# A graph layer's gathers in 342 slots and 61 rounds, a reordered first stage, and residual sums moved to DMAs

## What is computed

```python
# graph attention (GATv2), 4 heads of 64
h = rms_norm(xn) * rms_w @ W_down                   # 1250 x 256
src = concat(edge_src, arange(1250)); dst = concat(edge_dst, arange(1250))   # one edge to itself each
xl, xr = h @ Wl, h @ Wr
e = sum_d(att * leaky_relu(xl[src] + xr[dst]))      # per edge and head
alpha = softmax of e over the edges of one dst
gnn = segment_sum(alpha * xl[src], dst) @ W_up
# mixing without softmax
q, k, v = xn @ Wq.T + bq, xn @ Wk.T + bk, xn @ Wv.T + bv
mix = (q @ k.T * SCALE) @ v @ Wo.T + bo
x = x + gnn + mix
# feed-forward, weights and activations rounded to FP4 in blocks of 16
x = x + down(silu(gate(ln(x))) * up(ln(x)))
```

## Time and profile before

| | us |
|---|---|
| median of 3 runs | 925.71 (924.13 to 926.04) |
| profiled execution, its own time | 926.28 |
| its span, first to last instruction | 923.4 |
| TensorE busy | 854.8 (93%) |
| VectorE busy | 835.1 (90%) |
| ScalarE busy | 550.7 (60%) |
| GpSimd busy | 487.1 (53%) |

### The profile page before, as it was taken

How to read it: one execution, slowest core, us unless ns; L and a number is a source line. 1 busy time by engine, 2 the same in 40 slices (tenths; PEclk the granted TensorE clock), 3 DMA queues, 4 the chain that set the end, 5 groups by cost and what they waited for, 6 DMA issues and landing times.

```text
span 923.4 us, 9515 instructions
## 1 busy us (share of the span) xinstructions
PE 854.8 (93%) x2724; PEld 417.4 (45%) x2734; DVE 835.1 (90%) x1004; ACT 550.7 (60%) x1949; POOL 487.1 (53%) x512
## 2 busy tenths in 40 slices
PE   4999999999987999999999999999979988989664
PEld 3895455644433444444444444444434443444231
DVE  6989998779999999999999999999399689999994
ACT  3313123257767877879999978897388452343422
POOL 5200748577767767777777777877273100010101
PEclk8999999999997999999999999999999999999977
DMA  9322525553653533654335633339921210213124
GB/s 302 100 93 53 187 77 176 156 186 99 84 167 97 187 85 96 193 156 148 99 102 192 190 97 100 95 100 174 346 80 35 80 69 23 92 23 69 26 43 86
DMA packets 64850, 109.97 MB, mean 119 GB/s; under 512 B 29127, under 2 KB 35940, under 8 KB 64778
## 3 DMA queue, kind: packets, MB, share of 16 engines
q0 software_dynamic: 19856, 55.42, 24.3%
q1 hardware_dynamic: 44938, 53.92, 18.0%
HBM read 89.15 MB, written 17.17 MB: 115 GB/s over the span
## 4 chain that ended last, share of the span: by engine, by line
PE 72%; DVE 20%; SPq 2%; issue 2%; DMA 1%; ACT 1%; ACTq 0%; POOL 0%; DVEq 0%
PE acc L724 67%; DVE round_mem L1214 2%; DVE round_mem L1203 2%; SPq L515 2%; DVE round_mem L1204 2%; DMA big_b<-in_x 1%; PE turned L934 1%; DVE big_b L1556 1%; DVE round_mem L1207 1%; DVE round_mem L1208 1%; DVE z L1616 1%; PE turned L732 1%; DVE turned L1446 1%; PE turned L747 1%; DVE acc_sb L1454 1%
## 5 line engine op out<-in xcount | busy, mean ns | idle before, releaser
L552 POOL DMA_INDIRECT round_mem<-msg_table,idx x352 | 345.2, 981 | 102.1 <-issue 78.8
L1089 ACT ACTIVATE round_mem<-round_mem,pz 128x65 f32<-128x65 f32 x1408 | 353.9, 398 | 6.5 <-DVE acc_sb L1454 2.5
L724 PE MATMUL acc<-wslot,big_a 128*128 128x512 f32 x512 | 222.8, 597 | 7.9 <-DVE big_b L1411 7.9
L724 PEld LDWEIGHTS acc<-wslot,big_a 128*128 128x128 f32 x512 | 97.9, 192 | 131.2 <-issue 121.7
L1454 DVE TENSOR_REDUCE acc_sb<-round_mem 128x260 f32<-128x1820 f32 (+1 forms) x62 | 121.6, 1961 | 6.1 <-ACT round_mem L1089 4.0
L1079 ACT ACTIVATE pz<-z 128x7 f32<-128x7 f32 (+1 forms) x248 | 55.4, 296 | 107.9 <-DVE z L1621 107.7
L1446 DVE TENSOR_TENSOR turned<-round_mem,turned 128x1560 f32<-128x1560 f32 (+1 forms) x62 | 105.4, 1700 | 6.9 <-DMA round_mem<-msg_table,idx 4.6
L724 PE MATMUL acc<-wslot,big_b 128*128 128x512 f32 x256 | 110.0, 592 | 0.0
L724 PE MATMUL acc<-big_b,wslot 128*128 128x512 f32 x256 | 110.0, 592 | 0.0
L1616 DVE TENSOR_REDUCE z<-turned 128x24 f32<-128x1560 f32 (+1 forms) x62 | 105.1, 1695 | 2.1
L1614 DVE SCALAR_TENSOR_TENSOR turned<-turned,att_sb 128x1536 f32<-128x1536 f32 (+1 forms) x62 | 103.5, 1670 | 0.0
(11 more groups left out here) (232 smaller groups left out, 1022.9 us busy)
## 6 DMA issues: line engine op xcount, KB each, us to landing
big_b<-in_x SPq DMA_DIRECT2D x18, 512.0 KB, 9.9
round_mem<-msg_table,idx POOLq DMA_INDIRECT x352, 2.8
out_x<-big_b SPq DMA_DIRECT2D x9, 512.0 KB, 2.6
out_x<-acc_sb POOLq DMA_DIRECT2D x9, 512.0 KB, 5.4
wslot<-in_wv_t SPq DMA_DIRECT2D x2, 2048.0 KB, 9.2
wslot<-in_wk_t SPq DMA_DIRECT2D x2, 2048.0 KB, 9.4
wslot<-in_wo_t SPq DMA_DIRECT2D x2, 2048.0 KB, 9.4
wslot<-in_wq SPq DMA_DIRECT2D x2, 2048.0 KB, 9.9
```

The source lines that it names most:

```text
L552: pool.indirect_dma_start(xg[g % 4][:, j, :], None, msg_table, bass.IndirectOffsetOnAxis(idx[:, c, j0 + j:j0 + j + 1], 0)).then_inc(xg_in[ ...
L724: mm = nc.tensor.matmul(o(acc[:, n % 4, :]), a, b, start=first, stop=last)
L1089: ins = nc.scalar.activation(to[:, :, j], xg[g % 4][:, j, h * HR + 1:(h + 1) * HR], ACT.Copy, scale=pz[:, g % 2, j, h:h + 1])
```

## The change

Ten things change. (1) Slots: `CAPS`, so 342 slots in 61 rounds. (2) EARLY is 6 and not 7: two base groups move from before the tail into it. (3) The order of nodes is found by ScalarE (Sign with a sum, one instruction and a small one per block) between its takes of "lr"; each block's scatter starts when its rank is there. (4) VectorE and TensorE count the receivers earlier, and VectorE's order of weight pieces around that chain changes. (5) The small products "lin" go to a part of PSUM of their own and are no group. (6) GpSimd gathers the first block's receivers, then round 0's rows, then the other receivers. (7) The number of extra turns is worked out later in VectorE's order, by the same formula. (8) SP puts the bias row, and not x, into `base`; GpSimd adds x by accumulating DMAs (`add_x`) after its last gather. (9) GpSimd adds the mixing branch by accumulating DMAs (`lay_base`). (10) The plan of takes uses the round's size.

```diff
-EARLY = 7
+EARLY = 6
-CAPS = (54, 41, 38, 36, 34, 33, 32, 30, 28, 26)
+CAPS = (54, 40, 37, 35, 33, 32, 30, 29, 27, 25)
-PRODUCTS_AT, GROUP_STEP = 173.0, {"p0c": 2.0, "bias": 1.0}
-ROUND_0_AT, ROUND_STEP = 180.0, 8.5
+PRODUCTS_AT, GROUP_STEP = 172, {"p0c": 2.0, "bias": 1.0}
+ROUND_0_AT, SLOT_STEP, ROUND_OVER, TAKE_STEP = 160, 0.95, 2.2, 0.7
-BIAS_SUMS_AT, X_AT = 40, 54
+BIAS_SUMS_AT, X_AT = 43, 61
...
# SP
-            sp.wait_ge(acc_full, index_of["bias", 1] + 1)
+            sp.wait_ge(acc_taken["dve"], taken[index_of["bias", 1]])
             for c in range(C - 1):
-                sp.dma_start(base[:, c, :], x[c * NC:(c + 1) * NC, :]).then_inc(x_in[c], 16)
-            sp.wait_ge(mul_done, LAST + 1)
-            sp.dma_start(x_last, x[(C - 1) * NC:N, :]).then_inc(x_in[C - 1], 16)
+                sp.dma_start(base[:, c, :], bias_bc).then_inc(x_in[c], 16)
...
# GpSimd
-            pool.wait_ge(xr_out, 16)
+            pool.wait_ge(start_done, 1)
             for c in range(C):
                 pool.indirect_dma_start(neigh[:, c, :], None, src_table, ...)
             largest_weight(2)
+            pool.wait_ge(xr_out, 16)
+            receivers(0)
             pool.wait_ge(idx_done, 1)
             pool.wait_ge(table_out, 16)
             gather(0)
+            for c in range(1, C):
+                receivers(c)
+            pool.wait_ge(order_done, 2)
             rounds_over = pool.value_load(flags_i[0:1, 1:2], min_val=0, max_val=E)
             with pool.If(rounds_over > 0):
...
+                pool.dma_start(base[0:n, c, :], x[c * NC:c * NC + n, :], accum_op=ALU.add).then_inc(x_added[c], 16)
...
+                pool.dma_start(base[:, c, :].rearrange("p (k n) -> p k n", k=KB), base_at[c], accum_op=ALU.add).then_inc(base_added[c], 16)
...
# ScalarE
+            def rank(c):
+                nc.scalar.activation(is_above, key_row, ACT.Sign, scale=-1.0, bias=key_col[:, c:c + 1],
+                                     accum_out=rank_f[:, c:c + 1]).then_inc(ranked, 1)
+                act.wait_ge(ranked, c + 1)
+                nc.scalar.activation(rank_i[:, c:c + 1], rank_f[:, c:c + 1], ACT.Copy, scale=-0.5,
+                                     bias=0.5 * (NP - 1)).then_inc(rank_done, 1)
+            act.wait_ge(key_in, 32)
+            for c in range(3):
+                rank(c)
             for c in range(C):
                 take(index_of["lr", c])
+                if c + 3 < C:
+                    rank(c + 3)
...
# VectorE
-            for c in range(C):
-                step(nc.vector.tensor_scalar(is_above, key_row, key_col[:, c:c + 1], None, ALU.is_gt, ALU.add,
-                                             accum_out=rank_f[:, c:c + 1]))
-            nc.vector.tensor_copy(rank_i, rank_f).then_inc(rank_done, 1)
...
-            for c in range(min(LAST + 1 - X_AT, C - 2), C - 1):
-                add_bias(c)
-            dve.wait_ge(bias_added, C - 1)
-            for c in range(EARLY - 3):
-                add_base(c)
-            add_bias(C - 1)
```

More of the change, by code:

```diff
@@ L672, in rescale, with add_x, lay_base @@
                                         ALU.mult).then_inc(rescaled, 1)
+            def add_x(c):
+                n = rows(c)
+                if c < C - 1:
+                    pool.wait_ge(x_in[c], 32)
+                else:
+                    for i in range(C - 1):
+                        pool.wait_ge(x_in[i], 32)
+                pool.dma_start(base[0:n, c, :], x[c * NC:c * NC + n, :], accum_op=ALU.add).then_inc(x_added[c], 16)
+            def lay_base(c):
+                pool.wait_ge(acc_taken["act"], taken[index_of["base", ORDER["base"].index((c, 1))]])
+                pool.wait_ge(x_added[c], 16)
+                pool.dma_start(base[:, c, :].rearrange("p (k n) -> p k n", k=KB), base_at[c], accum_op=ALU.add).then_inc(base_added[c], 16)
             for g in range(1, LAST + 1):
@@ L686, in _ @@
                     send_attention(c)
+            for c in range(EARLY):
+                lay_base(c)
             def deviation_root(c):
@@ L956, in gps_layer @@
         round_of, freed, at = {}, {}, PRODUCTS_AT
-        for n in range(index_of["p", 0], len(groups)):
+        begun, n = ROUND_0_AT, index_of["p", 0]
+        for g, (_, _, slots, _, _) in enumerate(ROUNDS):
+            while n < len(groups):
+                kind, i, engine = groups[n]
+                full = max(at, freed.get(n - 4, 0)) + GROUP_STEP.get(kind, 7.0)
+                if full > begun:
+                    break
+                round_of[n], at = g, full
+                if kind == "base" and ORDER["base"][i][1] == 1:
+                    round_of[index_of["base", ORDER["base"].index((ORDER["base"][i][0], 0))]] = g
+                begun += TAKE_STEP if engine == "dve" else 0.0
+                freed[n] = begun + 0.8
+                n += 1
+            begun += ROUND_OVER + SLOT_STEP * slots
+            begun += 1.45 if g < KB or BIAS_SUMS_AT <= g < BIAS_SUMS_AT + KB else 0.0
+        for n in range(n, len(groups)):
             kind, i, _ = groups[n]
-            at = max(at, freed.get(n - 4, 0))
-            at += GROUP_STEP.get(kind, 7.0)
-            round_of[n] = max(0, math.ceil((at - ROUND_0_AT) / ROUND_STEP))
+            round_of[n] = LAST + 1
             if kind == "base" and ORDER["base"][i][1] == 1:
-                round_of[index_of["base", ORDER["base"].index((ORDER["base"][i][0], 0))]] = round_of[n]
-            freed[n] = max(at, ROUND_0_AT + round_of[n] * ROUND_STEP) + 1.5
+                round_of[index_of["base", ORDER["base"].index((ORDER["base"][i][0], 0))]] = LAST + 1
         def due(engine, g):
@@ L1550, in residual @@
             def residual(c, h):
-                if EARLY - 3 <= c < EARLY and (c, h) == min((i for i in x2_added if i[0] == c), key=x2_added.index):
-                    add_base(c)
+                if (c, h) == min((i for i in x2_added if i[0] == c), key=x2_added.index):
+                    if c < EARLY:
+                        dve.wait_ge(base_added[c], 16)
+                    else:
+                        dve.wait_ge(x_added[c], 16)
                 dve.wait_ge(x2_full, x2_made.index((c, h)) + 1)
@@ L1578, in sum_p0 @@
                 ins.then_inc(p0_summed, 1)
-            def add_bias(c):
-                n = rows(c)
-                dve.wait_ge(x_in[c], 32)
-                ins = nc.vector.tensor_tensor(base[0:n, c, :], x_last if c == C - 1 else base[:, c, :], bias_bc[0:n, :], ALU.add)
-                ins.then_inc(bias_added, 1)
-            def add_base(c):
-                dve.wait_ge(acc_taken["act"], taken[index_of["base", ORDER["base"].index((c, 1))]])
-                b = base[:, c, :].rearrange("p (k n) -> p k n", k=KB)
-                step(nc.vector.tensor_tensor(b, base_at[c], b, ALU.add))
-            assert round_of[index_of["bias", 1]] < X_AT
+            assert round_of[index_of["bias", 1]] + 3 < X_AT
             def sum_bias(k):
```

124 lines of the change are left out of this document (64 added, 60 removed).

## The result

The changed kernel takes **1182.17 us** (median of 4 runs, 1178.40 to 1183.14); the kernel before took 925.69 beside it. The ratio is 1.2801 (95% interval 1.2763 to 1.2840).

A forecast was written before the change was run, and what follows sets the result against it. TensorE and VectorE were taken as nearly full during the rounds. Round 0 at 432 after a 266 us turn, restart 465, last base group 967, first residual 971, tail 187: span 1158, forecast 1160 us, range 1125 to 1220.

The forecast's parts named there:

- The edges don't fit: Slots against caps: blocks 2 to 6, 8 and 9 each one short, so one extra turn runs through all ten blocks.
- no extra turn: Rival at the loop before round 0: slots miscounted, no turn runs, TensorE is the bound; 900 us, chance 0.08.
- The price of a block: One block's serial pass in the extra turn: 25.0 us of operations plus 1.5 for register waits, 26.5; 24 to 33.
- a block 38: Rival in the extra turn: register waits and fetches make each block 38 us; 1275 us, chance 0.07.
- Entering and leaving: Going into and out of the extra turn's loop: twice 5 us, between 0 and 15.
- VectorE reaches the loop: End of VectorE's first stage: at about 156 us instead of 174.3, since the ranks' 16 us leave VectorE.
- TensorE's restart: After the turn: TensorE goes on at 465 us, from round 0 at 432 plus 29 for three rounds plus 4.
- The products after it: TensorE from restart to last base group: 495 us for 72 groups, 4 for bias and small group, 3 for low clock.
- VectorE's rounds: VectorE from round 0 on: about 502 us, done at 938, beside TensorE, which ends later.
- "p" at 176: Start of TensorE's products: Gram begins some 2 us later because of ScalarE's ranks, so "p" begins at 176 us.
- The tail: From first residual to end of span: stays 187 us, with three add_base fewer and 4 us for two base groups.
- the DMA sums become the last wait: Rival at the first residual: it waits for bias, x and base sums on GpSimd's queue; +20, 1180 us, chance 0.05.

The follow-up runs named there:

- e1: Changed kernel with the number of extra turns forced to 0, so edges above the caps are left out of the result: 911.68 us, ratio 0.9866.
- e2: Changed kernel with the least caps that hold every edge (349 slots in 62 rounds): 910.54 us, ratio 0.9847.
- e3: Kernel before with only the new CAPS line of the change: 1185.63 us, ratio 1.2836.
- e6: e2 with one constant more, ROUND_0_AT = 172 for 160 in the plan of takes: 901.61 us, ratio 0.9762.
- e4: Changed kernel with the extra turn going only through the seven blocks short of a slot, every edge kept: 1102.08 us, ratio 1.1923.
- e8: Changed kernel with its turn and PRODUCTS_AT = 144 for 172, so p0 and p1 are taken in round 0, not round 3: 1169.00 us, ratio 1.2662.
- e9: e6 with EARLY 7, as before the change, in place of 6: 902.42 us, ratio 0.9787.
- e7: e6 with x, bias and mixing branch added by VectorE again as in the kernel before: 906.48 us, ratio 0.9811.

## Why the prediction was right

The direction, the mechanism and the size held: 1160 forecast, 1182 measured, inside 1125 to 1220. Point by point:

- **The edges don't fit: right.** e1, e2 and e3 show it from three sides. The rival "no extra turn" gave 900; e1, which is that rival, took 911.7. The rival took the plan to be on time, which e6 shows to be worth 8 us, and the tail to stay 187, where e1 has 190.9.
- **The price of a block: 26.5, measured 26.3** (27.15 for the first, 26.2 for each of the nine others), and 26.7 by e4. Two errors cancel by luck. The waits on register values, for which I added 1.5, cost nothing: gaps of a few hundredths of a us between VectorE's steps. The last reduction takes 3.4, where I took 2.05 from the rounds. The rival "a block 38" falls.
- **Entering and leaving: 10, measured next to nothing.** There are 0.21 us before the first instruction and 0.31 after the last. The 5.29 of the kernel before, where the loop is jumped over, are gone when it is run through, and are back as 6.46 in e2. The Trainium skill's rule (Runtime: NRT & Kernel Launch, Instruction fetch mechanics) is that a jump out of the fetched window waits for a fetch while straight code doesn't. The traces agree with it; they show where the gap stands, not the fetch itself. I had taken the sum to be 5 us lower by this rule; it was 10.
- **VectorE reaches the loop: 156, measured 171.** This step failed. I took the ranks' 16 us out and let the rest close up. But VectorE then waited: 5.1 for the places (at 108.7, forecast 106), 2.2 for GpSimd's maximum over the partitions, 7.2 for ScalarE's column sums (behind TensorE's Gram), and 4.2 for the receivers' rows, whose last gather GpSimd issued at 165.17, since they moved behind `gather(0)`; I had put their end near 150. So of 18 us only 3 came. The free entry (10) and the loop, 3 shorter than forecast, hide most of this: round 0 is at 434.9, against 432. That this is only 3 us off is luck.
- **TensorE's restart: 465, measured 469.7**, from p0 in round 3 as forecast. e8 shows why it is that late: the plan of takes, and not VectorE's time, held TensorE from 437 to 470.
- **The products after it: 502, measured 513.4.** This is the largest error that reaches the sum. I charged 3 us of low clock and nothing for late takes. The clock cost 2.5 (160 matmuls in 71.23 where 0.43 each would be 68.8), but TensorE waited 9.8 for ScalarE's takes of t1 and t2 on top, 6.1 of it ahead of the base groups. It waits so also without the turn (6.51 there in e2). The plan is part of the cause: with its constant moved, e6 waits 4.4 around the first base groups and nothing before them from 172 us on.
- **VectorE's rounds: about 502, measured 514.5** (434.9 to 949.4). The prediction's own terms make 510, not 502: the rounds before last 546 us (179.6 to 725.6), less 10, 2, 8.5 and 15.3. The gap from there to the end of the last base group is 33.7 us and not 29. Nothing of this reaches the sum, since TensorE came last.
- **"p" at 176, measured 172.7.** The 2 us later that I expected did not come; the products begin 1.7 sooner than before. TensorE then stands longer for it, and the sum doesn't change.
- **The tail: 187, measured 189.8.** The two base groups cost all of their 12.6 (e9), not 4, and the sums give back 4 to 5 (e7), about what I had for them. In steps: the other edits make the tail 6.2 shorter (e9), the two groups 12.6 longer (e6), and in the changed kernel it is 3.6 shorter than that, for a reason that is in part open. So the small error of 2.8 is luck.
- **The rival "the DMA sums become the last wait"** did not come. GpSimd issued the last `add_x` at 936.72 and the sum for block 3 at 957.07, each later one as soon as ScalarE had taken its groups. GpSimd of the changed kernel, in order of time, waits 12.20 and 12.38 for those takes, and its queue is otherwise free:

```profile
950.93 4.79 POOL L697 DMA_DIRECT2D big_b<-xhat_t  x3 [0.19 <-issue]
957.07 1.54 POOL L697 DMA_DIRECT2D big_b<-xhat_t  x1 [1.35 <-ACT xhat_t L1066]
970.80 1.54 POOL L697 DMA_DIRECT2D big_b<-xhat_t  x1 [12.20 <-ACT xhat_t L1066]
984.72 1.54 POOL L697 DMA_DIRECT2D big_b<-xhat_t  x1 [12.38 <-ACT xhat_t L1066]
```

The three sums of the first row, block 0's with them, were issued 31 us ahead of the first residual.

The measured 22 over the forecast are, in terms of the sum: round 0 at 434.9 for 432 (+3), the restart 2 later still, the products +11 and the tail +3, together 18.5 in the span. The rest is the way from span to median: 1.9 outside the span and 3.8 from the profiled run up to the median, where the forecast had 2.9 and 0.6 down.

Open is what exactly makes the tail of the changed kernel 3.6 us shorter than that of e6. TensorE's waits there are 24.8 us together against 27.3 in e6, of which 1.8 are one more wait for the attention output, which the changed kernel has not; the rest was not followed.

## What to carry to other kernels

When a size constant holds data, count first what the data need, off by one included: here ten slots, which TensorE's work hides anyway, were paid for with a 263 us detour that the profile of before doesn't contain. A fallback path that never ran can still be priced well from rows of the same shapes, if each link of its chain is written down (here with two errors of some 1.4 us a pass that cancel). And a plan of hard-coded times is part of every change that moves a stage: moving the stage without the constant gave away 8 of 22 us.

## What the runs showed of the hardware

- The same 1820 elements to 260 sums took VectorE 2.05 us in the rounds and 3.37 to 3.41 in each of the loop's ten passes. Both reductions have the same shape. In the rounds the slots of one sum lie side by side (`halves_of`), in the loop a whole gathered row apart (`xg_over`); that this is the cause was not tried by itself.
- Jumping over the loop costs VectorE 5.3 us in the kernel before and 6.4 to 6.5 in e1, e2 and e6; running into it costs 0.2. Here the jump stands on VectorE's way to round 0; what it would cost at a place where the engine waits anyway was not tried.
- A 269 us wait halves TensorE's granted clock (0.50 from 205 to 430 us, its lower level, 1.2 GHz), and coming back costs only 2.5 us in all. Both stretches have the columns of the earlier trace rows:

```profile
205.00:430.00 225.00, 0.00 (x0) 0.00 (x0) 112.50 (x152) 2.04 (x9) 60.56 (x77) 0.50 0.12 33
470.00:500.00 30.00, 30.00 (x66) 13.07 (x66) 29.48 (x26) 19.89 (x82) 22.70 (x25) 0.93 0.54 94
```
- The 1280-element comparison with a sum is no cheaper on ScalarE than on VectorE. On ScalarE it is 1.36 us, with 0.20 for its sum and 0.20 for the small one, and a rank holds the engine for 1.59 us from its start to the next take. On VectorE it is 1.545 and 0.08 for its sum, 1.58 from start to start. What the move brings is VectorE's time. The chain gets shorter by 13.9 us (the places arrive at 108.7 for 122.6): ScalarE's takes of "lr" stand between the ranks, one rank every 2.3 us.
